# Order of SyncE's weight loads at the change of stage in a graph layer: ring loads ahead of four early chunks

## The chip, the cores and the metric

The kernel runs on one core of a Trainium2 chip. The metric is device time in microseconds (us). Three runs of the kernel before took 329.73, 329.81 and 329.83 us; the median is 329.81.

## The reference, cut to what matters

Two residual layers over 256 nodes with 1024 features, in float32. Only what the kernel's work is made of is shown:

```
h   = relu(layernorm(x))                       # 256 x 1024
# 8448 edges (src, dst) in three kinds: 128 hh, 640 oo, the rest ho
e   = relu(concat(h[src], h[dst]) @ W_kind + b_kind)   # W_kind: 2048 x 1024
logit = e @ W_a + b_a
alpha = softmax of logit over the edges with the same dst
z   = segment_sum(alpha * h[src], dst)
x   = x + relu(concat(h, z) @ W_new + b_new)   # W_hn for 64 rows, W_on for 192
x   = x + relu(layernorm(x)) @ W.T + bias      # W: 8448 edge weights added into place
```

## The kernel before, in words

**Tables first, then gathers.** An edge's 2048-wide product is split: h @ top(W) and h @ bottom(W) are made once for all 256 nodes, stored to device memory as the tables p_ho and q_ho (later p_oo and q_oo), and each tile of 128 edges gathers its rows of p (by source) and of q (by destination). GpSimd (POOL) issues these gathers as indirect DMAs (L369 for p rows into the 12 slots of Gp, L383 for q rows into the 8 slots of Gq; 512 KB each). VectorE (DVE) adds the two (L668) and takes relu and the product with W_a with a running sum (L672). There are 65 such tiles; 66 with the hh tile, which has its own product.

**The stages.** (1) The ho tables: 16 chunks of weights (128 x 1024 each, SPLIT = 16), q = 0 to 15. ScalarE (ACT) rounds a chunk to its high half Wh (L413), VectorE makes the low half Wl (L621), and TensorE multiplies (`split_chunk`, L852). The eighth chunk completes p_ho, the sixteenth q_ho; ACT and DVE copy them out, and ACT's queue stores them (L428). (2) The hh tile: 16 chunks n = 0 to 15 by L963. Its first nine (PRE = 9) do not go through the ring of weights: they lie in other places, and are called early chunks here (L279). The first five of them lie in pre_f and pre_l; the last four, n = 5 to 8, lie in slots 4 to 7 of Gq, which until then hold the low halves Wl of chunks 12 to 15. (3) The jobs: 32 further steps of TensorE (L994, then L1016 to L1026), spread between the lots of edge tiles by a list (PACE), with the counting and placing products of each tile (L902). (4) The tail: softmax, sums, update, second layer.

**What sets the order around the change.** Each engine runs its own program in order, and so does SyncE (SP), which issues the weight loads. The ring W has five slots (WSLOTS). `load(q)` (L259) fills slot q % 5. For q up to 20 it waits for the low half of chunk q - 5 (semaphore s_lo, raised by L621); from q = 21 on for TensorE's use of the chunk that held the slot (s_wused). Chunks q = 16 to 22 of the ring are n = 9 to 15 of the hh tile. An early chunk n = 5 to 8 waits until s_wused is 13, 14, 15 or 16: until TensorE has done chunk 12, 13, 14 or 15 and left its Wl.

On POOL: twelve p gathers come first, then eight q gathers, then q and p in turn. The first q gather waits for q_ho in device memory (s_tab[1]). The q gathers i = 4 to 7 go into the places of the early chunks n = 5 to 8 and each waits until TensorE has used its own (`s_wused >= SPLIT + PRE_HEAD + i - HALVES + 1`). Later ones wait for DVE's sum of eight tiles before. On DVE, the first sum of gathered rows stands behind `few_counts` (L712 to L715).

Of the kernel before, what the change touches and what calls it, by code (L numbers as in the profile page):

```python
# [4 lines left out]
P = 128  # L5
# [38 lines left out]
HALVES = 4  # L44
# [5 lines left out]
SPLIT = 2 * KC  # L50
# [5 lines left out]
PRE_HEAD = 5  # L56
PRE = PRE_HEAD + 4
# [34 lines left out]
def uses_before(q):  # L92

    gone = q - WSLOTS
    if gone < SPLIT:
        return gone + 1
    return gone + PRE + 1 if gone < TOPS else TOPS + PRE + (gone - TOPS) // 2 + 1


def gnn_block(nc, x, edge_ids, edge_w, weights, bias_rows, w_a, b_a, l1_bias, out):  # L100
# [13 lines left out]
    with ctx:  # L114
# [4 lines left out]
        def shared(*makes):  # L119

            with ExitStack() as part:
                return [part.enter_context(nc.sbuf_tensor(*m)) for m in makes]

        _, hsT = shared(("t_low", [P, 2, NT, D], f32), ("hsT", [P, 2, KC, P], f32))
        x1, AT, Wd, h2, h2T = shared(("x1", [P, NT, D], f32), ("AT", [P, NT, N], f32), ("Wd", [P, NT, N], f32),
                                     ("h2", [P, NT, N], f32), ("h2T", [P, NT, N], f32))
# [6 lines left out]
                                  ("hTh", [P, KC, N], f32r), ("hTl", [P, KC, N], f32r))  # L135

        _, inv, off, Z, Ex, zT = shared(("gq_low", [P, FREED_Q % NQ, D], f32), ("inv", [P, NT, N], f32),
                                           ("off", [P, NT, N], f32), ("Z", [P, NT, N], f32), ("Ex", [P, NT, N], f32),
                                           ("zT", [P, KC, NH], f32))
        Gq = sb("Gq", [P, NQ, D], f32)  # L140
        RW = sb("RW", [P, WRING, 2, N], f32r)
        _, pre_l = shared(("rl_low", [P, D], f32), ("pre_l", [P, 2, D], f32))
        RL = sb("RL", [P, LRING, 2, N], f32r)

# [50 lines left out]
        pre = [pre_f[:, n, :] for n in (1, 2, 0)] + [pre_l[:, n, :] for n in range(2)]  # L195
# [17 lines left out]
        s_pre = [sem(f"early_w_in{n}") for n in range(PRE)]  # L213
        s_hi, s_lo, s_wused = sem("w_high_made"), sem("w_low_made"), sem("w_used")
# [37 lines left out]
        @block.sync  # L252
        def _(sp):
            for t in range(NT):
                sp.dma_start(xs[:, t, :], by_tile(x)[:, t, :]).then_inc(s_x[t], 16)

            def load(q):
                row = (q if q < SPLIT else q + PRE) * P
                sp.dma_start(W[:, q % WSLOTS, :], weights[row:row + P, :]).then_inc(s_w[q % WSLOTS], 16)  # L259

            sp.dma_start(ids[:, :, :], edge_ids).then_inc(s_ids, 16)
            for q in range(WSLOTS):
                load(q)
            sp.dma_start(ew[:, :], edge_w).then_inc(s_ew, 16)
            sp.wait_ge(s_const, 1)
            for p0 in (0, LOW0):
                sp.dma_start(brow[p0:p0 + BIASES, :], bias_rows).then_inc(s_small, 16)
            sp.dma_start(bar[:, :], b_a.broadcast_to((P, 1))).then_inc(s_small, 16)
            for q in range(WSLOTS, TOPS + 2 * LATE_TOP):
                if q - WSLOTS < SPLIT:  # L270
                    sp.wait_ge(s_lo, q - WSLOTS + 1)
                else:
                    sp.wait_ge(s_wused, uses_before(q))
                load(q)
                if HALVES < q < SPLIT and q % 2 and q // 2 - 2 < PRE_HEAD or SPLIT <= q < SPLIT + PRE - PRE_HEAD:
                    n = q // 2 - 2 if q < SPLIT else PRE_HEAD + q - SPLIT
                    if q >= SPLIT:
                        sp.wait_ge(s_wused, q - HALVES + 1)
                    sp.dma_start(pre[n], weights[(SPLIT + n) * P:(SPLIT + n + 1) * P, :]).then_inc(s_pre[n], 16)  # L279
                if q == 2 * WSLOTS:  # L280
                    sp.dma_start(wa[:, :], w_a.broadcast_to((P, D))).then_inc(s_wa, 16)

            def load_top(k):
                for q in range(TOPS + 2 * k, TOPS + 2 * k + 2):
                    sp.wait_ge(s_wused, uses_before(q))
                    load(q)

            def load_last(n):
                sp.wait_ge(s_used, FREED + n + 1)
                row = (TOPS + PRE + 2 * LAST_TOP + n) * P  # L290
                sp.dma_start(top_w[n], weights[row:row + P, :]).then_inc(s_top[n], 16)

            def load_hn(k):
                if k < HN_IN_GP:
                    sp.wait_ge(s_used, HN_AT + k + 1)
                else:
                    sp.wait_ge(s_wused, uses_before(TOPS + 2 * LAST_TOP + k - HN_IN_GP))
                sp.dma_start(hn_w[k], weights[(CHUNKS + PRE + k) * P:(CHUNKS + PRE + k + 1) * P, :]
                             ).then_inc(s_hn[k], 16)

            sp.wait_ge(s_sum, LATE_TILES)
            load_top(LATE_TOP)
            sp.wait_ge(s_sum, LAST_TILES)
            for n in range(len(LAST_SLOT)):
                load_last(n)
            sp.wait_ge(s_sum, HN_TILES)
            sp.wait_ge(s_hst, 16)
            sp.wait_ge(s_used, ROWS_AT + NT)
            sp.dma_start(rows_h, by_tile(h_rows)).then_inc(s_hr, 16)
            for k in range(KC):  # L310
                load_hn(k)
            sp.wait_ge(s_used, BREP_AT + 1)
            sp.dma_start(brep, l1_bias.broadcast_to((P, D))).then_inc(s_lb, 16)
            sp.wait_ge(s_tab[2], 16)
            sp.dma_start(x1[:, 1, :], x[P:N, :]).then_inc(s_xlo, 16)
            sp.dma_start(x1[:, 0, 0:HALF], x[0:P, 0:HALF]).then_inc(s_xlo, 16)
            for rows, place_of in ((lower, upper), (upper, lower)):
                sp.dma_start(x1[place_of, 0, HALF:D], x[rows, HALF:D]).then_inc(s_xlo, 16)
            sp.wait_ge(s_ylo, 1)
            sp.dma_start(out[0:P, N:HALF], x1[:, 0, N:HALF]).then_inc(s_out, 16)  # L320
            for rows, place_of in ((lower, upper), (upper, lower)):
                sp.dma_start(out[rows, HALF:D], x1[place_of, 0, HALF:D]).then_inc(s_out, 16)
            sp.wait_ge(s_ylo, 2)
            sp.dma_start(out[P:N, N:D], x1[:, 1, N:D]).then_inc(s_out, 16)
            for n, t in enumerate(TAIL):
                sp.wait_ge(s_o, n + 1)
                sp.dma_start(by_tile(out)[:, t, 0:N], x1[:, t, 0:N]).then_inc(s_out, 16)
            sp.wait_ge(s_out, 16 * (2 * NT + 2))
# [840 lines left out]
```

## Time and profile before

| | |
|---|---|
| runs, us | 329.73, 329.81, 329.83 |
| span of the profiled execution, us | 328.4 |
| TensorE (PE) busy | 309.0 us, 94% |
| VectorE (DVE) busy | 253.7 us, 77% |
| ScalarE (ACT) busy | 176.3 us, 54% |
| GpSimd (POOL) busy | 161.6 us, 49% |
| DMA | 122.06 MB, mean 372 GB/s |

The profile gives no time of the profiled execution other than its span; the median of the three timed runs is 1.41 us above that span. Busy shares are averages over stages with different limits. PE is busy nearly throughout, and the DMA rate stands at 400 to 420 GB/s from 98 us to 296 us.

### The profile page before, as it was taken

To read this page: it belongs to the slowest core of one execution; us is meant where nothing else is said; L and a number is where in the kernel's file an instruction comes from. 1 tells how busy PE (TensorE), PEld (TensorE's weight loads), DVE (VectorE), ACT (ScalarE), POOL (GpSimd) and SP (SyncE) were. 2 spreads that over 40 slices of the span, in tenths; PEclk is the share of its full clock that TensorE was granted. 3 is DMA by queue.
4 is the path that set the end of the run, shared out by engine and by line. 5 is a ranking of instruction groups with operands and counts; after the bars stand their busy time and mean duration, and the time that the engine had idled before them with its cause. 6 is when DMAs were issued, how large, how long until landed. Compare 5 with 4: busy or idle time off the path is not lost.

```text
span 328.4 us, 4177 instructions
## 1 busy us (share of the span) xinstructions
PE 309.0 (94%) x1376; PEld 197.6 (60%) x1381; DVE 253.7 (77%) x434; ACT 176.3 (54%) x437; POOL 161.6 (49%) x148
## 2 busy tenths in 40 slices
PE   0899999999999999999999999969998999999995
PEld 0687688845667666466575756646644554456543
DVE  4655446547999988999679898689988998998354
ACT  3854433182467654658656458545338396393202
POOL 3030057405877788787857888558788430000000
PEclk9999999999999999999999999987999899999999
DMA  7999979999999999999999999999999999999604
GB/s 255 402 399 407 368 247 316 399 402 334 366 357 413 409 410 409 409 408 410 419 408 411 408 409 409 416 412 408 410 408 411 410 406 409 402 409 410 246 0 128
DMA packets 34425, 122.06 MB, mean 372 GB/s; under 512 B 4058, under 2 KB 4570, under 8 KB 34404
## 3 DMA queue, kind: packets, MB, share of 16 engines
q0 software_dynamic: 19008, 69.21, 54.0%
q1 hardware_dynamic: 14004, 47.34, 37.3%
q10 hardware_dynamic: 1392, 5.24, 3.9%
q8 instruction: 11, 0.18, 0.2%
q14 instruction: 10, 0.08, 0.1%
HBM read 115.49 MB, written 6.29 MB: 371 GB/s over the span
## 4 chain that ended last, share of the span: by engine, by line
DMA 32%; PE 25%; POOL 22%; DVE 9%; issue 7%; ACT 3%; ACTq 0%; DVEq 0%
DMA Gq<-q_ho,ids 31%; PE psG L852 13%; POOL Gp L369 12%; POOL Gq L383 10%; PE psG L963 5%; DVE Gp L668 3%; PE psG L1071 2%; PE psG L1066 1%; DVE Gp L672 1%; DMA xs<-x 1%; PE psW L902 1%; ACT h L404 1%; DVE Wl L621 1%; ACT Wh L413 1%; DVE st L597 1%
## 5 line engine op out<-in xcount | busy, mean ns | idle before, releaser
L668 DVE TENSOR_TENSOR Gp<-Gp,Gq 128x1024 f32<-128x1024 f32 x65 | 79.3, 1221 | 24.3 <-DMA Gq<-q_ho,ids 21.6
L369 POOL DMA_INDIRECT Gp<-p_ho,ids x60 | 75.6, 1259 | 44.2 <-DMA p_ho<-T 24.3
L383 POOL DMA_INDIRECT Gq<-q_ho,ids x60 | 69.0, 1149 | 39.8 <-issue 14.9
L994 PE MATMUL psG<-W,hT 128*128 128x512 f32 x192 | 85.6, 596 | 0.0
L672 DVE SCALAR_TENSOR_TENSOR Gp<-Gp,wa 128x1024 f32<-128x1024 f32 x65 | 79.1, 1217 | 0.4
L478 ACT ACTIVATE RW<-ohs,ewh 128x256 fp32r<-128x256 f32 x66 | 33.2, 503 | 51.4 <-DVE ohs L659 47.1
L994 PEld LDWEIGHTS psG<-W,hT 128*128 128x128 f32 x192 | 35.7, 192 | 39.5 <-issue 39.0
L902 PE MATMUL psW<-RW,ohd 128*128 128x256 f32 x264 | 44.9, 293 | 0.1
L902 PEld LDWEIGHTS psW<-RW,ohd 128*128 128x128 f32 x264 | 36.7, 191 | 3.3 <-issue 2.9
L902 PE MATMUL psA<-RL,ohd 128*128 128x256 f32 x240 | 36.3, 296 | 2.2 <-ACT RL L488 1.6
L621 DVE TENSOR_TENSOR Wl<-W,Wh 128x1024 fp32r<-128x1024 f32 x16 | 19.6, 1223 | 22.2 <-ACT Wh L413 22.2
L902 PEld LDWEIGHTS psA<-RL,ohd 128*128 128x128 f32 x240 | 31.4, 196 | 7.6 <-ACT RL L488 6.9
L902 PE MATMUL psB<-ohs,ohd 128*128 128x256 f32 x132 | 32.2, 332 | 1.9 <-DVE ohd L661 1.9
L488 ACT ACTIVATE RL<-ohs,lg 128x256 fp32r<-128x256 f32 x66 | 32.9, 499 | 0.0
L488 ACT ACTIVATE RL<-ohs,lgl 128x256 fp32r<-128x256 f32 x66 | 32.7, 495 | 0.1
L478 ACT ACTIVATE RW<-ohs,ewl 128x256 fp32r<-128x256 f32 x66 | 32.7, 495 | 0.0
L902 PEld LDWEIGHTS psB<-ohs,ohd 128*128 128x128 f32 x132 | 21.1, 190 | 12.6 <-issue 10.3
L413 ACT CAST Wh<-W 128x1024 fp32r<-128x1024 f32 x16 | 16.8, 1050 | 18.1 <-PE psG L852 17.1
L659 DVE TENSOR_SCALAR ohs<-iota,idf 128x256 fp32r<-128x256 f32 x72 | 25.8, 358 | 0.0
L661 DVE TENSOR_SCALAR ohd<-iota,idf 128x256 fp32r<-128x256 f32 x72 | 25.6, 356 | 0.0
L852 PE MATMUL psG<-Wh,hTh 128*128 128x512 f32 x64 | 21.5, 418 | 1.4 <-DVE hTl L627 1.4
L852 PE MATMUL psG<-Wl,hTh 128*128 128x512 f32 x64 | 20.6, 405 | 0.0
(177 smaller groups left out, 357.7 us busy)
## 6 DMA issues: line engine op xcount, KB each, us to landing
W<-weights SPq DMA_DIRECT2D x63, 512.0 KB, 7.4
Gp<-weights SPq DMA_DIRECT2D x8, 512.0 KB, 10.1
Gq<-weights SPq DMA_DIRECT2D x4, 512.0 KB, 10.1
pre_f<-weights SPq DMA_DIRECT2D x3, 512.0 KB, 7.4
xs<-x SPq DMA_DIRECT2D x2, 512.0 KB, 3.8
h_rows<-h ACTq DMA_DIRECT2D x1, 1024.0 KB, 6.8
pre_l<-weights SPq DMA_DIRECT2D x2, 512.0 KB, 7.2
p_ho<-T ACTq DMA_DIRECT2D x2, 512.0 KB, 4.7
```

What stands on the lines that cost most here:

```text
L369: nc.gpsimd.indirect_dma_start(out=Gp[:, i % NP, :], out_offset=None, in_=p_oo if t <= OO_TILES else p_ho, in_offset=bass.IndirectOffsetOn ...
L383: nc.gpsimd.indirect_dma_start(out=Gq[:, i % NQ, :], out_offset=None, in_=q_oo if t <= OO_TILES else q_ho, in_offset=bass.IndirectOffsetOn ...
L478: last = nc.scalar.activation(RW[:, w % WRING, half, :], ohs[:, (first + i) % RING, :].bitcast(f32), ACT.Copy, scale=val[:, t:t + 1].bitca ...
L488: return nc.scalar.activation(RL[:, n % LRING, half, :], ohs[:, (ENTRY[g] + i) % RING, :].bitcast(f32), ACT.Copy, scale=val[:, g % 2, i:i ...
L621: nc.vector.tensor_tensor(Wl[:, q % HALVES, :], W[:, q % WSLOTS, :], Wh[:, q % HALVES, :].bitcast(f32), ALU.subtract).then_inc(s_lo, 1)
L659: nc.vector.tensor_scalar(ohs[:, n % RING, :], iota[:, :], idf[:, tile, 0:1], None, ALU.is_equal).then_inc(s_ohs, 1)
L661: nc.vector.tensor_scalar(ohd[:, n % RING, :], iota[:, :], idf[:, tile, 1:2], None, ALU.is_equal).then_inc(s_ohd, 1)
L668: nc.vector.tensor_tensor(Gp[:, i % NP, :], Gp[:, i % NP, :], Gq[:, i % NQ, :], ALU.add).then_inc(s_sum, 1)
L672: nc.vector.scalar_tensor_tensor(out=Gp[:, i % NP, :], in0=Gp[:, i % NP, :], scalar=0.0, in1=wa[:, :], op0=ALU.max, op1=ALU.mult, accum_ou ...
L852: ins = nc.tensor.matmul(psG[:, 2 * t + half, :], lhs[:, k, cols], rhs[:, s, half * HALF:(half + 1) * HALF], start=not opened and k == 0 a ...
L902: ins = nc.tensor.matmul(bank[:, c, :], ohd[:, slot, c * P:(c + 1) * P], m, start=False, stop=False, skip_group_check=True)
L994: last = nc.tensor.matmul(psG[:, 2 * t + half, :], hT[:, k, t * P:(t + 1) * P], W[:, s, half * HALF:(half + 1) * HALF], start=u != 1 and k ...
```

## The change

In stage 2, SP's loads and early chunks stood in turn: load 16, early chunk 5, load 17, early chunk 6, load 18, early chunk 7, load 19, early chunk 8, load 20. Now the loads 16 to 20 come first, and then the early chunks 5 to 8. What each one waits for is the same as before: `min(SPLIT + n - PRE_HEAD - HALVES + 1, SPLIT)` is 13, 14, 15 and 16 for n = 5 to 8, and load q still waits for the low half of chunk q - 5. The order of the loads up to 15, the five first early chunks, all places and all bytes are as before. The helper load_pre holds the DMA that stood in the loop.

```diff
+            def load_pre(n):
+                sp.dma_start(pre[n], weights[(SPLIT + n) * P:(SPLIT + n + 1) * P, :]).then_inc(s_pre[n], 16)
+
...
                 load(q)
-                if HALVES < q < SPLIT and q % 2 and q // 2 - 2 < PRE_HEAD or SPLIT <= q < SPLIT + PRE - PRE_HEAD:
-                    n = q // 2 - 2 if q < SPLIT else PRE_HEAD + q - SPLIT
-                    if q >= SPLIT:
-                        sp.wait_ge(s_wused, q - HALVES + 1)
-                    sp.dma_start(pre[n], weights[(SPLIT + n) * P:(SPLIT + n + 1) * P, :]).then_inc(s_pre[n], 16)
+                if HALVES < q < SPLIT and q % 2 and q // 2 - 2 < PRE_HEAD:
+                    load_pre(q // 2 - 2)
+                elif q == SPLIT + HALVES:
+                    for n in range(PRE_HEAD, PRE):
+                        sp.wait_ge(s_wused, min(SPLIT + n - PRE_HEAD - HALVES + 1, SPLIT))
+                        load_pre(n)
```

## Rows read from the trace of the kernel before

**Rows 1.** Page, the chain that ended last, by line.

```profile
DMA Gq<-q_ho,ids 31%; PE psG L852 13%; POOL Gp L369 12%; POOL Gq L383 10%; PE psG L963 5%; DVE Gp L668 3%; PE psG L1071 2%; PE psG L1066 1%; DVE Gp L672 1%; DMA xs<-x 1%; PE psW L902 1%; ACT h L404 1%; DVE Wl L621 1%; ACT Wh L413 1%; DVE st L597 1%
```

**Rows 2.** Waits of VectorE, 76 to 300 us: waited for, total us, times, longest.

```profile
DVE Gp L668 <- DMA Gq<-q_ho,ids: 21.6, 22, 3.3
```

**Rows 3.** Busy time by stretch; the last three columns are clock, DMA share, GB/s.

```profile
45.30:56.00 10.70, 10.70 (x54) 8.85 (x53) 4.74 (x8) 4.60 (x6) 8.60 (x7) 1.00 0.80 260
66.00:76.30 10.30, 10.30 (x33) 5.17 (x32) 6.11 (x2) 7.49 (x18) 0.00 (x0) 1.00 1.02 407
76.30:96.00 19.70, 19.70 (x92) 12.79 (x92) 17.53 (x29) 8.51 (x22) 15.72 (x14) 1.00 0.95 337
118.00:285.40 167.40, 162.26 (x717) 99.75 (x718) 144.89 (x255) 98.49 (x269) 108.55 (x89) 0.97 1.03 410
```

**Rows 4.** Timeline of SyncE: loads 16, early 5, 17 and 20 (start, us).

```profile
42.00 0.33 SPq L259 DMA_DIRECT2D W<-weights  x1
...
55.76 0.33 SPq L279 DMA_DIRECT2D Gq<-weights  x1
56.13 0.43 SPq L259 DMA_DIRECT2D W<-weights  x1
...
64.29 0.49 SPq L259 DMA_DIRECT2D W<-weights  x1
```

**Rows 5.** Timeline of VectorE: low halves of chunks 12 and 15.

```profile
44.10 1.23 DVE L621 TENSOR_TENSOR Wl<-W,Wh 128x1024 fp32r<-128x1024 f32 x1 [2.13 <-ACT Wh L413]
...
53.69 1.23 DVE L621 TENSOR_TENSOR Wl<-W,Wh 128x1024 fp32r<-128x1024 f32 x1 [1.96 <-ACT Wh L413]
```

**Rows 6.** Timeline of ScalarE's queue: the second store of q_ho.

```profile
65.02 0.33 ACTq L428 DMA_DIRECT2D q_ho<-T  x1
```

**Rows 7.** DMA queues, 66 to 76.3 us: packets, MB, share of 16 engines.

```profile
q1 hardware_dynamic: 445, 1.63, 39.1%
...
q10 hardware_dynamic: 288, 1.05, 25.0%
```

**Rows 8.** Timeline of GpSimd: q gathers 0, 6, 7, 8 and 9.

```profile
76.32 0.93 POOL L383 DMA_INDIRECT Gq<-q_ho,ids  x1 [14.38 <-DMA q_ho<-T]
...
85.05 0.94 POOL L383 DMA_INDIRECT Gq<-q_ho,ids  x1 [0.30 <-PE psG L963]
86.29 1.29 POOL L383 DMA_INDIRECT Gq<-q_ho,ids  x1 [0.31 <-issue]
87.89 0.94 POOL L383 DMA_INDIRECT Gq<-q_ho,ids  x1 [0.30 <-issue]
...
90.73 0.94 POOL L383 DMA_INDIRECT Gq<-q_ho,ids  x1 [0.30 <-issue]
```

**Rows 9.** Timeline of VectorE: end of few_counts, first sum of gathered rows.

```profile
78.20 0.75 DVE L715 TENSOR_SCALAR off_few<-off_few,bar 128x1024 f32<-128x1024 f32 x1
81.05 1.22 DVE L668 TENSOR_TENSOR Gp<-Gp,Gq 128x1024 f32<-128x1024 f32 x1 [2.10 <-DMA Gq<-q_ho,ids]
```

**Rows 10.** Timeline of TensorE: hh chunks 5 and 8, both from Gq.

```profile
76.45 1.88 PE L963 MATMUL psG<-Gq,hsT 128*128 128x512 f32 x4
...
83.01 1.88 PE L963 MATMUL psG<-Gq,hsT 128*128 128x512 f32 x4
```

**Rows 11.** Page, DMA issues: count, size, median us from issue to landing.

```profile
Gq<-weights SPq DMA_DIRECT2D x4, 512.0 KB, 10.1
```

**Rows 12.** Timeline of TensorE's weight loads near the last edge tiles.

```profile
291.10 0.53 PEld L902 LDWEIGHTS psA<-RL,ohd 128*128 128x128 f32 x4 [0.16 <-ACT RL L488]
...
296.62 0.53 PEld L902 LDWEIGHTS psA<-RL,ohd 128*128 128x128 f32 x4 [0.26 <-ACT RL L488]
```

**Rows 13.** Timeline of TensorE: a wait late in the jobs, and L1016 twice.

```profile
252.10 0.97 PE L863 MATMUL psG<-biases,selr 64*128 64x512 f32 x2 [0.69 <-ACT T L433]
...
253.64 3.45 PE L1016 MATMUL psG<-W,hT 128*128 128x512 f32 x4
...
262.05 1.88 PE L1016 MATMUL psG<-W,hT 128*128 128x512 f32 x4
```

## The prediction, made before the changed kernel was run

> **What bounds the kernel now.** I read the chain that ended last first [rows 1]. Its largest item is DMA, the gathers of q rows; POOL's issuing of both kinds of gathers follows. TensorE is busy 94% of the span, yet its largest item there, L852, belongs to the opening stage. So from some point on the stream of gathers sets the end. VectorE's waits say the same: 22 times its sum L668 stood for a q gather, 21.6 us in all [rows 2]. The table by stretch says why: from 118 to 285.4 us the DMA engines move 410 GB/s, where 66 to 76.3 us shows 407 with other queues in play [rows 3]. About 410 is thus the ceiling of this kernel. Ahead of it there are holes: 260 GB/s from 45.3 to 56 us, 337 from 76.3 to 96 us [rows 3]. Only bytes that go into such holes earlier can bring the last gather forward.
>
> **What the change moves.** No instruction and no byte is added or removed; four loads move past early chunks in SP's queue. Load 16 went out at 42.00 [rows 4]. Behind it SP stood until 55.76 for chunk 12 on TensorE, and load 17 followed at 56.13; load 20 was last at 64.29 [rows 4]. Loads 17 to 20 wait only for the low halves of chunks 12 to 15. These are made at 44.10 + 1.23 = 45.33 (first) and 53.69 + 1.23 = 54.92 (last), two more between them [rows 5]. So load 17 goes from 56.13 to 45.3, and load 20 from 64.29 to 54.9: 9.4 to 10.8 us earlier each. Early chunk 5 could go at 55.76, later than 54.92 + 0.5 for issuing load 20, so the early chunks are issued as before. I cost them at nothing: TensorE takes chunk 5 at 76.45 [rows 10], 20.7 us after its issue, and the median landing is 10.1 us [rows 11]. Some 10 us of cover would have to go before TensorE waits. The ring chunks 16 to 20 are used after chunk 8, behind 84.9, so that they come earlier is worth nothing by itself either. Load 21 waits for TensorE as before.
>
> **Step 1, the backlog.** Four loads are 4 x 0.524 = 2.10 MB. From 45.3 to 56 us the engines moved 260 x 10.7 = 2.78 MB; at the 407 GB/s of a full stretch they would move 4.35, so 1.57 MB fit in, 1.57 / 0.407 = 3.9 us of later traffic. By the other column, a busy share of 0.80, only 20% of 10.7 = 2.1 us are free [rows 3]. These are my two bounds. What they relieve is the pile-up from 56 to 76 us, in which the store of q_ho lies: its second half is issued at 65.02 [rows 6], and the first q gather goes at 76.32, released by it after POOL's wait of 14.38 us [rows 8]. The engines move 407 GB/s until then and less after [rows 3], so I read the store's end as the end of the pile-up. It moves to 72.4 or 74.2.
>
> Here a rule speaks against the change. In those 10.3 us the stores' queue moved 1.05 MB and SP's queue 1.63 [rows 7]; the store had neither priority nor last place. The Trainium skill, "DMA: Bandwidth & Descriptors", section "Queues, rings and completion order", says that each DMA engine goes round the queue rows that have work, one packet of each in turn. By it alone the store's end depends on how many queues are busy and not on how much stands behind them, and would not move while SP's queue still has work; the sum would be zero. By that rule, the trace agrees only in part, since 25.0% and 39.1% are no equal shares [rows 7]. The rule gives the second case below.
>
> **Step 2, POOL and VectorE.** The first sum comes at 81.05, 4.7 us behind the first q gather's issue at 76.32, after a wait of 2.10 us; VectorE had finished few_counts at 78.95 [rows 8, 9]. With the store at 74.2 or earlier the gather is there by 78.9, so both bounds of step 1 give the same: VectorE starts 2.1 us earlier, then few_counts ends last, which hangs on TensorE and does not move. POOL's gathers 0 to 3 come earlier by as much as the store, but gather 7 needs the place of early chunk 8, which TensorE leaves at 83.01 + 1.88 = 84.9 at the latest; before, gather 6 started at 85.05 for want of nothing else but its turn [rows 8, 10]. So gather 7 moves from 86.29 to about 85.05, by 1.24 us. If it then takes the 0.94 us of its neighbour and not its own 1.29, gather 8 moves from 87.89 to 86.29, by 1.60 [rows 8]. I take 1.5: the shorter duration is the one that most of its neighbours have, with 0.1 off for its release.
>
> **Step 3, what reaches the end.** POOL issues one p and one q gather per 90.73 - 87.89 = 2.84 us, 1.05 MB, or 369 GB/s [rows 8]. Bytes issued 1.5 us earlier are 0.55 MB, and these go into the hole before 96 us, where 410 - 337 leaves 1.4 MB free [rows 3]. Where the stream then runs at 410 GB/s, it is ahead by 0.55 / 0.410 = 1.35 us. Bounds: nothing, if the store does not move; 1.24 x 0.9 = 1.1 us and 1.60 x 0.9 = 1.4 us by step 2; 2.1 us if VectorE, not the DMA engines, sets the pace. I take 1.4 us, since VectorE's waits stretch over the whole stretch [rows 2] and say that DMA does. TensorE's jobs between 118 and 285.4 us have 167.4 - 162.26 = 5.1 us of idle time [rows 3], more than 1.4, and the late wait is for ACT, which follows the logits [rows 13]; so I let TensorE follow. The tail follows the last logit.
>
> Sum: the profiled span of 328.4 becomes 327.0; with the 1.41 us by which the median of the runs stands above it, **328.4 us**.
>
> **The rivals.** (a) *The store does not move*, by even sharing among the queues, or what is gained goes into POOL's wait for TensorE. For it: the store's 25% [rows 7], and TensorE's release at 84.9, which leaves only 1.24 us [rows 8, 10]. Against it: the rate falls off when the store ends, so all queues were drained together [rows 3]. Time: 329.8. The change would then not do for the gathers what it does for the loads.
>
> (b) *TensorE ends last.* Near the end TensorE waited 0.16 and 0.26 us for ACT's products [rows 12]: it was a mere 0.4 us ahead. It comes there from a long run without waits, whose start is at a lower clock: four L1016 products take 3.45 us at 253.64 and 1.88 at 262.05, so the first are for the most part at the 1.2 GHz level and the others at 2.4, behind a stretch with waits such as that of 0.69 us [rows 13]. Over 118 to 285.4 us the granted clock is 0.97, which is 0.03 x 167.4 = 5.0 us of full clock lost [rows 3]. If the shifted waits put two more such spells, 3.14 us, into that last run, TensorE's end is 3.14 - 0.4 = 2.7 us behind VectorE's: 328.4 + 2.7 = 331.1, slower than before. It begins to eat the gain at 0.4 us of clock lost beyond now and turns it into a loss at 1.8. Against it: the waits get shorter, not longer, if VectorE is ahead.
>
> (c) *VectorE's 2.1 us arrive in full*, since POOL and VectorE run in one rhythm from 82 us on and the queues hold many tiles: 329.81 - 2.1 = 327.7. For it: POOL's turn is 2.84 us, the same as VectorE's. Against it: TensorE's hold on gather 7.
>
> **How the numbers follow.** About 0.2%, 0.66 us, is what a measurement of this kernel can tell from no change. The forecast with 1.4 us, between 0.7 and 1.8, has 0.49; (c) 0.12; (a), with lesser gains and small losses of clock, 0.25; (b) or another loss of that size 0.14. Faster: 0.49 + 0.12 = 0.61; same 0.25; slower 0.14. The forecast's own range is 328.0 to 329.1. For 8 in 10 the range has to take in (c) and most of (a): 327.2 to 330.0, which leaves out (b) and little below.
>
> **What would show it.** Right: load 17 issued near 45.3, the early chunks still at 55.8 to 64; 45 to 56 us well above 260 GB/s; the first q gather at 72 to 74; the first sum near 79; gather 8 near 86.3; from 96 us on 410 GB/s as before, and each later sum 1.4 us earlier, to the last. Wrong: a first q gather still near 76 (a); an unchanged gather 8 in spite of it; a longer spell of low clock after 253 us and a TensorE that waits for nothing at 291 and 296 (b). A wait of TensorE before hh chunk 5 would say that the early chunks were not free. The forecast fails at once if the first sum moves by 2 us and the last does not move.

## The result, and the profile after

The changed kernel ran 20 times with a median of 328.20 us (326.92 to 329.82), beside 20 runs of the kernel before with 329.9 us: ratio 0.9955, 95% interval 0.9933 to 0.9977. That is 1.5 us faster, between 0.8 and 2.2. The forecast was 328.4. A second comparison, below, gave 0.9974 (0.9946 to 1.0003), so the gain is likelier near 1 us than near 2. In the last comparison of the experiments many executions, those of the kernel before too, were disturbed and took up to 343 us; ratios and means leave these out.

The profiled execution has a span of 327.4 us (328.4 before). Line numbers behind the change are four higher: L668 is L672 now, L383 is L387, L852 is L856. First SyncE's timeline of the changed kernel, ring loads 16, 17 and 20 and early chunk 5 (L262):

```profile
42.08 0.33 SPq L259 DMA_DIRECT2D W<-weights  x1
45.46 0.33 SPq L259 DMA_DIRECT2D W<-weights  x1
...
55.04 0.33 SPq L259 DMA_DIRECT2D W<-weights  x1
55.85 0.33 SPq L262 DMA_DIRECT2D Gq<-weights  x1
```

Load 17 went from 56.13 to 45.46 and load 20 from 64.29 to 55.04; early chunk 5 stays at 55.85 [rows 4]. The loads do what the text of the change says. The changed kernel by stretch (start:end, length, busy time of each engine; clock, DMA share, GB/s last):

```profile
45.30:56.00 10.70, 10.70 (x55) 8.82 (x54) 4.76 (x8) 4.60 (x6) 8.69 (x7) 1.00 0.90 323
66.00:76.30 10.30, 10.30 (x32) 5.15 (x32) 6.02 (x2) 7.58 (x19) 0.93 (x1) 1.00 0.96 389
76.30:96.00 19.70, 19.70 (x94) 12.87 (x93) 18.80 (x32) 8.91 (x23) 15.36 (x14) 1.00 0.95 321
96.00:118.00 22.00, 17.46 (x75) 12.48 (x75) 14.12 (x26) 11.38 (x33) 14.31 (x14) 0.81 1.03 411
118.00:285.40 167.40, 165.59 (x743) 101.27 (x741) 152.09 (x267) 102.81 (x282) 104.27 (x91) 0.99 1.03 410
```

The first hole went from 260 to 323 GB/s, 0.67 MB more; the other one, from 76.3 us, is wider than before, 321 for 337 [rows 3]. By queue, the first hole had 2.76 MB of GpSimd's gathers and 0.02 MB of SP's loads before; it has 2.11 MB of gathers and 1.35 MB of loads now. From 96 us on the rate is as before: 410. Then GpSimd's q gathers 0, 7 and 8:

```profile
75.31 0.93 POOL L387 DMA_INDIRECT Gq<-q_ho,ids  x1 [13.28 <-DMA q_ho<-T]
...
85.25 1.16 POOL L387 DMA_INDIRECT Gq<-q_ho,ids  x1 [0.43 <-PE psG L967]
86.71 0.94 POOL L387 DMA_INDIRECT Gq<-q_ho,ids  x1 [0.30 <-issue]
```

and VectorE's timeline: the end of few_counts, the first sum, the last sum.

```profile
78.29 0.75 DVE L719 TENSOR_SCALAR off_few<-off_few,bar 128x1024 f32<-128x1024 f32 x1
79.88 1.23 DVE L672 TENSOR_TENSOR Gp<-Gp,Gq 128x1024 f32<-128x1024 f32 x1 [0.83 <-DMA Gq<-q_ho,ids]
...
291.61 1.22 DVE L672 TENSOR_TENSOR Gp<-Gp,Gq 128x1024 f32<-128x1024 f32 x1
```

The first q gather is 1.0 us earlier than before, the first sum 1.17, gather 8 1.18 [rows 8, 9], and the last sum 1.04 (292.65 before). In this pair of profiles the lead at the head is near the lead at the end; in the next pair it is not. Nor is it constant between them: VectorE stands still in this profile from 106.6 us on (`remote` is what the trace can only name as another core or an unknown queue),

```profile
114.49 0.35 DVE L663 TENSOR_SCALAR ohs<-iota,idf 128x256 fp32r<-128x256 f32 x1 [7.88 <-remote]
```

and its sum 12 is at 121.81 us, 6.7 us later than before. By sum 40 it is ahead again (209.66 for 214.06), while the DMA engines went on at 411 GB/s. But the second profile of the kernel before has its sum 40 at 207.68, 6.4 us from its first, and its last sum 3.1 us from it: sums in the middle say nothing of the change. Whether this standstill belongs to the change had to be tested. Last, the queues of the changed kernel from 66 us to the end of q_ho's store at 75.3 (packets, MB, share of 16 engines):

```profile
q1 hardware_dynamic: 304, 1.07, 28.4%
q10 hardware_dynamic: 288, 1.05, 27.6%
```

### The profile page after: what moved, and what is told of

The parts are those of the page before. It is cut to its first block, busy times and chain, and to the rows that moved or that the text cites. A ratio compares the mean times of both kernels' runs of the same rounds, so it can differ in the third digit from the quotient of the medians.

```text
span 327.4 us, 4182 instructions
## 1 busy us (share of the span) xinstructions
PE 307.0 (94%) x1381; PEld 197.7 (60%) x1381; DVE 253.1 (77%) x434; ACT 176.2 (54%) x437; POOL 154.3 (47%) x148
## 2 busy tenths in 40 slices
DMA packets 34425, 122.06 MB, mean 373 GB/s; under 512 B 4058, under 2 KB 4570, under 8 KB 34404
## 4 chain that ended last, share of the span: by engine, by line
PE 53%; DMA 16%; DVE 12%; ACT 6%; POOL 5%; issue 5%; another core or an unknown queue 2%; ACTq 0%; DVEq 0%; POOLq 0%
PE psG L998 17%; PE psG L856 13%; DMA Gq<-q_ho,ids 9%; PE psA L906 5%; PE psW L906 5%; DMA q_oo<-T 3%; DMA q_ho<-T 3%; POOL Gp L373 3%; DVE Gp L672 3%; PE psB L906 3%; POOL Gq L387 3%; PE psG L1075 2%; DVE Gp L676 2%; PE psG L1020 2%
## 5 line engine op out<-in xcount | busy, mean ns | idle before, releaser
L373 POOL DMA_INDIRECT Gp<-p_ho,ids x60 | 69.7, 1162 | 52.2 <-DMA p_ho<-T 25.4
L387 POOL DMA_INDIRECT Gq<-q_ho,ids x60 | 69.5, 1158 | 39.5 <-issue 15.9
L672 DVE TENSOR_TENSOR Gp<-Gp,Gq 128x1024 f32<-128x1024 f32 x65 | 79.4, 1221 | 9.9 <-DMA Gq<-q_ho,ids 5.9
L906 PE MATMUL psW<-RW,ohd 128*128 128x256 f32 x264 | 45.6, 295 | 3.6 <-issue 1.9
L906 PEld LDWEIGHTS psW<-RW,ohd 128*128 128x128 f32 x264 | 37.4, 193 | 7.1 <-issue 5.4
L906 PE MATMUL psA<-RL,ohd 128*128 128x256 f32 x240 | 35.2, 295 | 0.9 <-ACT RL L492 0.7
L417 ACT CAST Wh<-W 128x1024 fp32r<-128x1024 f32 x16 | 16.8, 1050 | 18.0 <-PE psG L856 17.1
L856 PE MATMUL psG<-Wh,hTh 128*128 128x512 f32 x64 | 21.5, 418 | 1.4 <-DVE hTl L631 1.4
L856 PE MATMUL psG<-Wl,hTh 128*128 128x512 f32 x64 | 20.6, 404 | 0.0
## 6 DMA issues: line engine op xcount, KB each, us to landing
W<-weights SPq DMA_DIRECT2D x63, 512.0 KB, 13.3
```

The costliest lines, as they stand in the source:

```text
L373: nc.gpsimd.indirect_dma_start(out=Gp[:, i % NP, :], out_offset=None, in_=p_oo if t <= OO_TILES else p_ho, in_offset=bass.IndirectOffsetOn ...
L387: nc.gpsimd.indirect_dma_start(out=Gq[:, i % NQ, :], out_offset=None, in_=q_oo if t <= OO_TILES else q_ho, in_offset=bass.IndirectOffsetOn ...
L672: nc.vector.tensor_tensor(Gp[:, i % NP, :], Gp[:, i % NP, :], Gq[:, i % NQ, :], ALU.add).then_inc(s_sum, 1)
L856: ins = nc.tensor.matmul(psG[:, 2 * t + half, :], lhs[:, k, cols], rhs[:, s, half * HALF:(half + 1) * HALF], start=not opened and k == 0 a ...
L906: ins = nc.tensor.matmul(bank[:, c, :], ohd[:, slot, c * P:(c + 1) * P], m, start=False, stop=False, skip_group_check=True)
```

## The experiments

All kernels were timed in five rounds beside the kernel before. Theory A: the gain is the earlier start of the stream of gathers. Theory B: the gain is the bytes that go into holes of the DMA engines' work. Theory C came up on the way: an earlier opening of TensorE fills the same hole. The names in brackets are those of the table at the end. "Give or take" is a 95% interval of a difference of means.

**Both kernels again** ("again"). No edit.

> The kernel before once more, as a second profile and as a measure of how far two equal programs differ. All theories: ratio 1.000 within about 0.002. The profiled stream: first q gather near 76.3 us, first sum near 81.0, gather 8 near 87.9. If its later stream (sums 12 to 40) differs by microseconds from the first profile of the same program, then sums in the middle of the span say nothing about the change, and only the head (to 100 us) and the last sums may be compared.

> The changed kernel once more, beside the kernel before. All theories: 0.9955 again, within its interval of 0.993 to 0.998, so 1.5 us faster. The head of the profile repeats: store of q_ho ends near 75.3 us, first sum 79.9, gather 8 at 86.7. If the standstill of ScalarE, VectorE and TensorE at 100 to 114 us in the first profile of the changed kernel belongs to the change (theory: DMA traffic of the ring loads stands before something), it is here again; if it comes by chance, it is absent or elsewhere.

Kernel before: ratio 1.0009 (0.9979 to 1.0038), median 329.15 of 12 runs. Changed kernel: 0.9974 (0.9946 to 1.0003), 327.89. The difference of their means is 0.87 us, give or take 0.8. The gain is there, at 0.26% rather than 0.45%, and this second interval alone does not exclude zero.

The profiles, however, had another head than the first ones: spans of 325.3 (kernel before) and 325.5 us (changed). The difference begins in the opening. TensorE's second pair of products in the first profile of the kernel before,

```profile
14.27 1.05 PE L852 MATMUL psG<-Wl,hTh 128*128 128x512 f32 x2
```

and the same pair in the second profile of the same program:

```profile
13.85 0.63 PE L852 MATMUL psG<-Wl,hTh 128*128 128x512 f32 x2
```

The same products take 1.05 us in one execution, until 17.7 us, and 0.63 in the other; from one pair to the next it is 0.85 and 0.47 us. That is nearly the ratio of the 1.2 GHz level to the 2.4 GHz level, but the column of the granted clock shows 1.00 in both, so that the clock is the reason is not shown. In both TensorE waited 1.4 or 1.5 us ahead of them, behind its transposes. It gives the hh stage a start at 66.3 or at 64.2 us. So the first pair of profiles (late opening) and this one (early opening) are two comparisons: in the late one the span fell by 1.0 us, in the early one it rose by 0.2. A reason can be read from the early kernel before, 76.3 to 96 us:

```profile
76.30:96.00 19.70, 19.70 (x91) 12.64 (x91) 15.36 (x27) 7.60 (x20) 15.43 (x15) 1.00 1.02 402
```

Here the engines have no hole behind 76 us, since the pile-up is still there when the gathers join it. In the early changed kernel it is 345 GB/s: the pile-up has gone, and POOL's issuing is the likely limit, as eight q gathers of 0.524 MB in the 12.05 us from 73.00 to 85.05 are 348 GB/s.

This pair also shows what the first sum is worth. The first sum and the last in the early kernel before, and the last in the early changed kernel:

```profile
81.30 1.23 DVE L668 TENSOR_TENSOR Gp<-Gp,Gq 128x1024 f32<-128x1024 f32 x1 [4.34 <-DMA Gq<-q_ho,ids]
...
289.51 1.22 DVE L668 TENSOR_TENSOR Gp<-Gp,Gq 128x1024 f32<-128x1024 f32 x1
```

```profile
289.75 1.22 DVE L672 TENSOR_TENSOR Gp<-Gp,Gq 128x1024 f32<-128x1024 f32 x1
```

The changed kernel's first sum is at 78.21, 3.1 us earlier, and its last 0.24 us later. A lead of VectorE at the head is not a lead at the end. The bytes moved by 96 us go with the last sum: 35.20 MB in the kernel before, 35.11 in the changed one.

**Hold the gathers back by 1 us** (changed kernel; hold_q):

```diff
                     pool.wait_ge(s_tab[1], 32)
+                    nc.gpsimd.memset(spare[:, :], 0.0)
```

> The changed kernel with one GpSimd memset of about 1.0 us (128x1024, bf16, of a place that nothing reads) between the end of q_ho's store and the first q gather; the ring loads stay early. Theory A (the gain is the lead of the stream of gathers, 1.2 us at gather 8): the lead is gone, gather 8 back at 87.7 to 87.9, and the time is that of the kernel before, ratio 0.999 to 1.001. Theory B (the gain is that ring loads and stores are out of the way, whatever the gathers do): ratio stays at 0.995 to 0.997.

Ratio 0.9991 (0.9962 to 1.0021); 0.70 us (give or take 0.8) slower than the changed kernel in the same comparison. Its profile has a late opening, q gather 0 at 76.28 and gather 8 at 88.53 us (87.89 before), 289 GB/s behind 76.3 us and a span of 328.6. The ring loads are early, the gathers are not, and no gain is left in the profile. That is for theory A, but weakly: the interval of the times also admits a part of B, the 0.70 us are not clear of zero, and the hold did more than was meant. Gather 8 came 1.8 us later than in the changed kernel's first profile, 0.6 us later than in the kernel before, and fewer bytes had moved by 96 us (33.66 MB for 33.85), so that theory B, counted in bytes by then, expects no gain either.

**Ring loads late instead of early** (kernel before; early chunks 6 to 8 ahead of load 17, and loads 17 to 20 behind q_ho's store; late_ring):

```diff
                 if q - WSLOTS < SPLIT:
                     sp.wait_ge(s_lo, q - WSLOTS + 1)
+                    if q == SPLIT + 1:
+                        for n in range(PRE_HEAD + 1, PRE):
+                            sp.wait_ge(s_wused, SPLIT + n - PRE_HEAD - HALVES + 1)
+                            sp.dma_start(pre[n], weights[(SPLIT + n) * P:(SPLIT + n + 1) * P, :]).then_inc(s_pre[n], 16)
+                        sp.wait_ge(s_tab[1], 32)
...
-                if HALVES < q < SPLIT and q % 2 and q // 2 - 2 < PRE_HEAD or SPLIT <= q < SPLIT + PRE - PRE_HEAD:
+                if HALVES < q < SPLIT and q % 2 and q // 2 - 2 < PRE_HEAD or q == SPLIT:
```

> The kernel before with the ring loads 17 to 20 put behind the early chunks and held until q_ho is stored: out of the pile-up on its other side, into the hole behind 76 us instead of that ahead of 56. Theory A (lead of the gathers; what matters is what stands beside q_ho's store): the store ends at 71 to 73 us, first sum at 79.0, gather 8 at 86.3 to 86.7, and the time is 1.2 to 1.8 us below before, ratio 0.994 to 0.997. Theory B (bytes have to move in the hole ahead of 56 us): no gain, ratio 0.999 or above, since the 2.1 MB now compete with the gathers from 76 us on. The hh chunks 9 to 12 are needed from 87 us on and should land near 80 to 84.

Ratio 1.0018 (0.9987 to 1.0049), and 1.46 us (give or take 0.8) slower than the changed kernel: theory A alone, which wanted 0.994 to 0.997, falls. GpSimd's q gathers 0 and 8 in this kernel:

```profile
73.00 0.94 POOL L388 DMA_INDIRECT Gq<-q_ho,ids  x1 [10.69 <-DMA q_ho<-T]
...
84.83 0.94 POOL L388 DMA_INDIRECT Gq<-q_ho,ids  x1 [0.30 <-issue]
```

and gather 8 in the changed kernel's second profile, where gather 0 is at 73.00 as well:

```profile
85.05 0.94 POOL L387 DMA_INDIRECT Gq<-q_ho,ids  x1 [0.30 <-issue]
```

POOL issues as early in the one as in the other. But the first sum of the late-ring kernel comes 2.6 us later, 80.83 for 78.21 us. First the late ring, then the changed kernel:

```profile
80.83 1.22 DVE L673 TENSOR_TENSOR Gp<-Gp,Gq 128x1024 f32<-128x1024 f32 x1 [4.04 <-DMA Gq<-q_ho,ids]
```

```profile
78.21 1.23 DVE L672 TENSOR_TENSOR Gp<-Gp,Gq 128x1024 f32<-128x1024 f32 x1 [1.41 <-DMA Gq<-q_ho,ids]
```

The 2.1 MB of ring loads now stand beside the q gathers, the engines run full from 76.3 us (403 GB/s) and yet have moved 0.70 MB less by 96 us than in the changed kernel: the hole from 45.3 to 56 us stayed at 223 GB/s, against 311. The hh chunks were not late: TensorE is busy for all of 76.3 to 96 us. Beside the early kernel before, the first sum is 0.5 us earlier and the last 2.1 us later (291.63 for 289.51).

**A warm opening** (b_warm, a_warm), TensorE put to work on zeros ahead of its first products, to take the change of openings out of the comparison:

```diff
             pe.wait_ge(s_const, 1)
+            for _ in range(14):
+                nc.tensor.matmul(psG[:, 0, :], zero[:, 0:P], zero[:, :], start=True, stop=True, skip_group_check=True)
...
             everyone = slice(0, P)
+            for _ in range(4):
+                clear(psG[:, 0, :])
```

> The kernel before, with TensorE kept at work on zeros ahead of its first products (14 short products before 8 us, 4 more behind the transposes), so that the opening L852 products do not start at the lower clock, as they do in some profiles (the pair of L852 takes 1.05 us until 17.7 us, and 0.62 in others; the hh stage then begins at 66.3 or 64.2 us). Both theories: hh stage at 64.2 in every profile, less spread between runs. Theory B (the end is set by the bytes that the DMA engines have moved by 96 us, 1 MB for 2.4 us) and the profile of the kernel before with the early head (325.3 us, 402 GB/s in 76 to 96 us): about 1.5 us below the kernel before, ratio 0.994 to 0.997.

> The changed kernel with the same warm opening. Theory A (ring loads out of the way give the gathers a lead whatever the opening): 1.2 to 1.6 us below b_warm. Theory C (the change and an early opening fill the same hole in the DMA engines' work; the two profiles with an early opening, kernel before and changed kernel, had 325.3 and 325.5 us): level with b_warm within 0.4 us. The bytes moved by 96 us should tell which one in the profiles: A wants 0.5 MB more than b_warm.

Kernel before, warm: 0.9983 (0.9952 to 1.0014), median 328.11. Changed, warm: 0.9956 (0.9937 to 0.9976), 327.45. Changed less before: 0.68 us, give or take 0.56. All profiles had the early opening. The spread of the changed kernel's runs fell (standard deviation 0.93 us in its own repeat, 0.48 here), that of the kernel before hardly (1.07 and 0.85), and in the second warm pair below they are 0.86 and 1.14, so less spread is not shown. Bytes by 96 us: 34.76 and 35.07 MB; theory A wanted 0.5 MB between them and found 0.3. The forecast of 1.5 us for the warm opening itself was missed: 0.17%, 0.6 us.

**The same two levers under a warm opening** (hold_warm, late_warm). The edits are those of above.

> The changed kernel, warm opening, and one GpSimd memset of 1.0 us ahead of the first q gather. If the rate of the DMA engines from 76 us on hangs on POOL's start, this costs 0.8 to 1.0 us against a_warm. If q gathers 4 to 7 wait for TensorE anyway, it costs under 0.4.

> Ring loads 17 to 20 behind the early chunks and behind q_ho's store, warm opening. Theory B (bytes by 96 us): the hole ahead of 56 us stays empty, and what goes in behind 73 us delays the q gathers beside it; 1.0 to 2.0 us slower than a_warm, as late_ring was 1.5 us slower than the changed kernel. The q gathers' lead at issue (gather 8 near 84.9) is the same as in a_warm, so if issue alone counted the two would be level.

Held: 0.9964 (0.9943 to 0.9985), 0.38 us (give or take 0.41) slower than the changed warm kernel, less than the microsecond by which POOL was held: gather 8 moved by 0.73, from 85.43 to 86.16. The interval takes in zero. Late ring: 0.9999 (0.9973 to 1.0025), 1.58 us (give or take 0.50) slower than the changed warm kernel and 0.90 (0.65) slower than the warm kernel before, although its gather 8 was first of all, at 84.26. Where the loads go is worth more than when POOL issues. Its profile, however, does not show the expected picture: the hole from 45.3 to 56 us was not empty but at 313 GB/s, all of it gathers, and the hole came from 66 to 76.3 us (327 GB/s, against 418 in b_warm). By 96 us it had moved 34.83 MB, no less than b_warm, with the same span of 326.2. So the 0.90 us between these two kernels stand in the timed runs, and no profile shows where they arise.

**Fewer bytes** (kernel before, warm; less_warm): ring loads 17 and 18 load only 64 of 1024 columns.

```diff
-                sp.dma_start(W[:, q % WSLOTS, :], weights[row:row + P, :]).then_inc(s_w[q % WSLOTS], 16)
+                cols = slice(0, 64) if q in (SPLIT + 1, SPLIT + 2) else slice(0, D)
+                sp.dma_start(W[:, q % WSLOTS, cols], weights[row:row + P, cols]).then_inc(s_w[q % WSLOTS], 16)
```

> The kernel before, warm opening, with the ring loads 17 and 18 cut to their first 64 columns: 0.98 MB less to move in the pile-up, nothing else changed (the hh products then use old values of the other columns). Theory B, straight: the end falls by what the DMA engines have less to do, 0.98 / 0.41 = 2.4 us below b_warm (the fit over ten profiles says 2.35 us for each MB). If instead only the lead of the first q gathers counts, it is the lead that 0.98 MB fewer beside q_ho's store give and POOL passes on, at most 1.2 us. If TensorE sets the end, nothing.

Ratio 0.9959 (0.9932 to 0.9986), with 0.9979 for the warm kernel before in the same comparison: 0.2%, 0.7 us, and 1.1 us (give or take 0.9) by the means, not 2.4. Straight theory B falls too, by a narrow margin. The profile: 369 GB/s from 66 to 76.3 us instead of 418, 330 from 76.3 us instead of 379, and gather 8 at 86.40, later than in the warm kernel before (85.77). The 0.98 MB were missing from the pile-up, and nothing took their place; they became a hole. They did not move the end of q_ho's store either: gather 0 is at 74.58 us, 74.54 in b_warm. That comparison is not clean, as the store's second half was issued 0.7 us later here (63.77 for 63.06).

**Early chunks 7 and 8 behind q_ho's store** (changed, warm; split_warm):

```diff
                         sp.wait_ge(s_wused, min(SPLIT + n - PRE_HEAD - HALVES + 1, SPLIT))
+                        if n == PRE - 2:
+                            sp.wait_ge(s_tab[1], 32)
                         load_pre(n)
```

> The changed kernel, warm opening, and early chunks 7 and 8 held until q_ho is stored (they are used at 79 to 83 us). The hole of 66 to 76 us in a_warm (360 GB/s) is filled by them while the q gathers start earlier: store ends at 71.5 instead of 73.8, gather 8 at 84.3 to 84.8 instead of 85.4. Theory B with bytes by 96 us up by 0.2 to 0.3 MB: 0.5 to 0.7 us below a_warm. If the two chunks stand before the first q gathers, as the ring loads did in late_ring, the first sum does not come earlier and it is level with a_warm or up to 0.5 us slower.

Ratio 0.9949 (0.9913 to 0.9984), level with 0.9948 of the changed warm kernel beside it. The store ended at 71.26 and gather 8 was issued at 84.41, as forecast, but the first sum came at 78.70 (78.60 in a_warm): the two chunks now stood beside the first q gathers, as the forecast had allowed. The bytes by 96 us are the same, 35.09 and 35.07 MB, and so is the time.

**The warm pair again** (b_warm2, a_warm2).

> b_warm once more, to halve the variance of the pair. Ratio to the kernel before 0.996 to 1.000; profile as b_warm within 1 us of span and 5 GB/s in the mean to 96 us.

> a_warm once more. The change under a warm opening was worth 0.7 us (plus or minus 0.6) in the first pair. Theory A with the full lead: 1.2 us or more below b_warm2. Theory C (the holes are partly filled already once the opening is early): 0.3 to 1.0.

Ratios 0.9979 (0.9942 to 1.0017) and 0.9948 (0.9915 to 0.9982): 0.31% between them, 1.0 us; by the means it is 1.23 us, give or take 0.95. The two warm pairs together say 0.8 us, give or take 0.5. Theory C's 0.3 to 1.0 fits this; theory A's 1.2 or more is not excluded by it.

**What the profiles have in common.** The mean rate from 0 to 96 us, as MB moved by 96 us, and the span:

| kernel | opening | MB by 96 us | span, us |
|---|---|---|---|
| hold_q | late | 33.66 | 328.6 |
| before | late | 33.85 | 328.4 |
| changed | late | 34.29 | 327.4 |
| late_ring | early | 34.41 | 327.4 |
| hold_warm | early | 34.74 | 326.6 |
| b_warm | early | 34.76 | 326.2 |
| late_warm | early | 34.83 | 326.2 |
| a_warm | early | 35.07 | 325.0 |
| split_warm | early | 35.09 | 325.9 |
| changed, again | early | 35.11 | 325.5 |
| before, again | early | 35.20 | 325.3 |

A straight line through the eleven falls 2.3 us for each MB (correlation 0.98) and misses none by more than 0.7; the engines' own pace, 410 GB/s, makes 2.4. Counted as bytes left at 96 us, less_warm fits as well: its 33.5 MB and 0.98 never loaded give 326.9 by that line, measured 326.6.

Much of this line is bookkeeping. All eleven move 122.06 MB; at 410 GB/s the rest takes until 308 to 312 us, and each span lies 16.8 to 17.8 us behind that. So it says that the rate from 96 us on and the tail were the same in all, and that an execution which has moved more by 96 us ends earlier. It does not say what made the bytes move, nor does it hold where the rate is not kept: the profiles of b_warm2 and a_warm2 had moved 34.74 and 35.16 MB by 96 us and took 341.0 and 334.9 us, at 400 and 403 GB/s from 118 to 285.4 us. And one profile is one execution: late_warm lies beside b_warm in the table and was 0.90 us slower in the timed runs.

What the timed runs show of the theories is this: with POOL issuing as early or earlier, the ring loads in the late place cost 1.5 and 1.6 us against the early place (late_ring, late_warm), so their place matters. How much of the gain is the gathers' lead stays open, as both holds have intervals that take in zero.

The lowest ratios are those of the change with the warm opening: 0.9956 and 0.9948 to the kernel before. Against the changed kernel's 0.9955 and 0.9974, in other comparisons, that is no difference that can be told.

## Why the prediction was right

**What bounds the kernel** was right and is what the table rests on: gathers at the DMA engines' pace of 410 GB/s from 96 us on.

**What the change moves** was right to 0.2 us for each load, and the cover of the early chunks held: no wait of TensorE ahead of hh chunk 5.

**Step 1 had the wrong size.** I gave the end of q_ho's store 2.1 to 3.9 us; it moved by 1.0 (76.32 to 75.31), and by 1.6 between the two profiles with an early opening (74.60 to 73.00). Two things were taken too high. The hole took in 0.67 MB and not 1.57. The loads did move 1.35 MB there, but GpSimd's gathers moved 0.65 MB less beside them than before (2.11 for 2.76), and these came back in the pile-up: its queue had 1.50 MB in 10.3 us before and 1.72 in 9.3 now. The prediction had the loads in the idle time alone and not in the gathers' way. And the store's end was not the end of the pile-up: SP's queue shrank from 1.63 MB in 10.3 us to 1.07 in 9.3, while the stores' queue had 1.05 MB in both, at a share of 27.6% for 25.0% [rows 7]. The Trainium skill, "DMA: Bandwidth & Descriptors", section "Queues, rings and completion order", has each engine take a packet in turn from every queue row with work. By that rule, the trace agrees this far: a shorter queue beside the store should help it only once that queue has run dry. In split_warm SP's queue was empty from 66 us on; the store had 40.0% of the engines and ended at 71.26, 2.5 us before a_warm's. In less_warm SP's queue had 0.98 MB less in all but was not dry (43.8% from 66 to 74.5 us), and the end did not move. But in the changed kernel SP's queue ran dry late, and from 73 to 75.3 us GpSimd's queue had 77.9% and the store's 19.9%. I used the rule as a rival that gives nothing, and used drained queues for the sum; the measured 1.0 us lies between. After the store, the rate fell to 143 GB/s from 75.3 to 76.3 us, and to 389 over 66 to 76.3: the engines ran out of work before POOL gave them any.

**Step 2 followed from it.** VectorE's first sum came 1.17 us earlier and not 2.1, since a gather and not few_counts ended last (a wait of 0.83 us). Gather 7 at 85.25 us was on TensorE's release as said, and gather 8 gained 1.18 us for the 1.5 that I took.

**Step 3 held with these numbers put in**: 1.18 us of gathers at 369 GB/s are 0.44 MB, as in the profile (33.85 to 34.29), and 0.44 / 0.410 = 1.1 us; the last sum moved by 1.04 and the span by 1.0. That the two numbers of MB are equal is in part chance, since the hole behind 76.3 us did not fill, as the step has it, but widened by 0.3 MB; more had moved ahead of it. That 1.4 us was so near to the first measurement of 1.5 is luck in part; the four comparisons together say about 1. The signs were not all as named: sums in the middle did not keep a lead, and in the pair with an early opening the first sum moved by 3.1 us and the last did not, which the prediction names as its failure. What the step did not have is a second limit: where TensorE's opening is early there was no hole behind 76 us to fill, the pile-up filled it, and the change trades one hole for another. One pair of profiles shows that, and the warm pair, which opens early too, shows it less (0.3 MB and 1.2 us of span for the change); that the timed runs divide in this way was not shown, as they come without profiles.

**The rivals.** (a) was right on the sharing and wrong on its result. (b) did not come: at 252.17 us the four L1020 products (L1016 before) take 1.98 us, against 3.45 [rows 13], and TensorE has a granted clock of 0.99 from 118 to 285.4 us. Yet TensorE did come last in this one profile, by the chain of waits: 53% of it is TensorE, the stretch from the standstill to 204 us and the last jobs. With a margin of 0.4 us either can be named, and the five profiles in which TensorE is named are those with a standstill (below). (c) fell with the first sum.

## What to carry to other kernels

Where the second half of a kernel is one transfer at the ceiling, count the bytes that are moved when that stretch starts: each MB there is its time at the ceiling, and a lever on the head is better weighed by it than by the wait that it shortens. Moving loads out of a pile-up paid here where there was an earlier hole for them and other transfers to take their place; the late ring lacked the one, the shortened loads the other. Count also whose transfers already run in that hole: the loads took 0.65 MB of it from the gathers. And repeat the profile before reading 1 us from it: two profiles of one program differed by 3.1 us here. The whole gain, 0.3 to 0.45%, is about one standard deviation of single runs.

## What the runs showed of the hardware

**One program, two openings.** The products from 13.3 to 17.7 us ran at about half pace in the first profiles of both kernels and in that of hold_q, and at full pace in the second ones and in late_ring, with nothing changed ahead of them. With work for TensorE put ahead of them, all eight profiles had full pace. 2 us at the head stood beside about 3 in the span in the two profiles of the kernel before; in the timed runs the warm opening was worth 0.6 us.

**A standstill of three engines.** VectorE's gap of 7.9 us at 106.6 us stands in the changed kernel's first profile. Like gaps are in split_warm (5.1 us, in three parts) and a_warm2 (6.7 us at 106.1), and in b_warm2 (6.8 us at 98.9) and less_warm, which have SP's order of before:

```profile
114.38 0.35 DVE L660 TENSOR_SCALAR ohs<-iota,idf 128x256 fp32r<-128x256 f32 x1 [8.09 <-remote]
```

It is absent in the other nine profiles, of either order, so it does not hang on the change. In the changed kernel's first profile ScalarE stood for 7.0 us until 107.1 and TensorE had gaps without a named releaser; the granted clock from 96 to 118 us is 0.81 there and 0.77 in less_warm. What started it is open; no run here was made for it. In three of the five no cost of it shows in the span, which lies on the line of the others: the DMA engines went on at 411 GB/s, and VectorE later waited 5.9 us for q_ho gathers where it had waited 21.6 [rows 2]. The other two are b_warm2 and a_warm2, with 341.0 and 334.9 us; what part the standstill has in that is not shown.
